# Rotary turn of q in an attention stage: sine parts swapped by transfers and summed on GpSimd, q once in the scores

## The reference

```python
h = rmsnorm(x) * ln1_w                   # queries from x
q = rope(h @ Wq)                         # 16 heads of 64
k = rope(rmsnorm(ctx) * ln1_w @ Wk)      # 4 heads of 64
v = rmsnorm(ctx) * ln1_w @ Wv
x = x + softmax(q k^T / 8 + mask) v @ Wo # 4 query heads share a k head
m = rmsnorm(x) * ln2_w
x = x + (silu(m @ Wgate) * (m @ Wup)) @ Wdown
rope(a) = a * cos + rotate_half(a) * sin # rotate_half(a) = [-a2, a1]
```

## Time and profile before

| | |
|---|---|
| median of 3 runs | 496.73 us (496.45 to 497.52) |
| the profiled execution's own time | 496.65 us |
| its span, first to last instruction | 494.7 us |
| TensorE busy | 445.4 us (90%) |
| VectorE busy | 381.2 us (77%) |
| ScalarE busy | 299.3 us (60%) |
| GpSimd busy | 273.8 us (55%) |

### The profile page before, as it was taken

How to read it: one execution, slowest core, us unless ns; L and a number is a source line. 1 busy time by engine, 2 the same in 40 slices (tenths; PEclk the granted TensorE clock), 3 DMA queues, 4 the chain that set the end, 5 groups by cost and what they waited for, 6 DMA issues and landing times.

```text
span 494.7 us, 16947 instructions
## 1 busy us (share of the span) xinstructions
PE 445.4 (90%) x6872; PEld 353.1 (71%) x6872; DVE 381.2 (77%) x918; ACT 299.3 (60%) x725; POOL 273.8 (55%) x332
## 2 busy tenths in 40 slices
PE   4698899999999999989989768999999999999876
PEld 4466666666666676679877656888888888878664
DVE  6699877688988888968889878877686876767632
ACT  2377676768676877666863655576656665544431
POOL 6464887579867787965644374454353535421210
PEclk9799999999999999999999999999999999999998
DMA  8960000000000000000000000000000000000000
GB/s 291 240 234 3 2 3 3 2 3 3 1 3 2 3 3 3 3 1 2 1 1 3 2 1 4 3 12 2 14 1 13 1 3 14 1 13 1 14 2 21
DMA packets 12421, 11.54 MB, mean 23 GB/s; under 512 B 5177, under 2 KB 10297, under 8 KB 12345
## 3 DMA queue, kind: packets, MB, share of 16 engines
q1 hardware_dynamic: 11624, 9.01, 6.7%
q10 hardware_dynamic: 720, 1.45, 0.8%
HBM read 9.42 MB, written 1.05 MB: 21 GB/s over the span
## 4 chain that ended last, share of the span: by engine, by line
PE 51%; DVE 24%; issue 14%; POOL 5%; ACT 4%; DMA 1%; DVEq 0%; POOLq 0%; ACTq 0%
DVE negm L1249 8%; PE ps L618 5%; DVE blocks L1240 5%; PE ps L634 4%; PE ps L656 4%; PE ps L448 4%; PE ps L734 4%; PE ps L466 3%; PE ps L532 2%; PE ps L545 2%; PE ps L611 2%; PE ps L626 2%; PE ps L496 2%; PE ps L664 2%; PE ps L408 2%
## 5 line engine op out<-in xcount | busy, mean ns | idle before, releaser
L1249 DVE TENSOR_REDUCE negm<-ps 128x8 bf16<-128x512 f32 x96 | 59.6, 683 | 24.9 <-PE ps L448 24.8
L833 ACT ACTIVATE p<-ps 128x512 f32<-128x512 f32 x96 | 54.7, 595 | 27.5 <-PE ps L456 26.4
L839 ACT ACTIVATE shared<-ps 128x512 f32<-128x512 f32 x96 | 57.0, 601 | 21.8 <-PE ps L466 20.4
L1742 POOL TENSOR_TENSOR wide<-wide,cv 128x1024 f32<-128x1024 f32 x24 | 45.5, 1896 | 32.8 <-ACT wide L823 32.8
L466 PE MATMUL ps<-cst,p 128*128 128x128 f32 x384 | 58.4, 276 | 0.4 <-ACT shared L839 0.4
L1795 POOL TENSOR_TENSOR probs<-p,rc 128x512 f32<-128x512 f32 x32 | 33.4, 1057 | 43.2 <-DVE rc L1535 43.1
L1669 POOL TENSOR_TENSOR rstd<-veps,neghalf 128x2 f32<-128x2 f32 x40 | 29.3, 732 | 46.4 <-DVE veps L1285 28.2
L466 PEld LDWEIGHTS ps<-cst,p 128*128 128x128 f32 x384 | 44.2, 141 | 11.5 <-issue 9.4
L1028 ACT ACTIVATE late<-ps 128x512 f32<-128x512 f32 x32 | 17.3, 594 | 34.3 <-PE ps L757 34.3
L618 PE MATMUL ps<-shared,wq 128*128 128x256 f32 x128 | 31.3, 386 | 5.2 <-ACT shared L976 3.4
L634 PE MATMUL ps<-wo,late 128*128 128x128 f32 x256 | 31.5, 276 | 4.0 <-ACT late L1028 3.8
(11 more groups left out here) (204 smaller groups left out, 1150.9 us busy)
## 6 DMA issues: line engine op xcount, KB each, us to landing
late<-in_mask_l SPq DMA_DIRECT2D x2, 512.0 KB, 11.0
result<-x_all SPq DMA_DIRECT2D x8, 128.0 KB, 1.8
x_all<-in_x_tok SPq DMA_DIRECT2D x1, 768.0 KB, 6.6
...
wa<-in_wa SPq DMA_DIRECT2D x1, 512.0 KB, 8.4
w<-in_w SPq DMA_DIRECT2D x2, 256.0 KB, 7.5
wq<-in_wq SPq DMA_DIRECT2D x1, 512.0 KB, 7.2
```

The lines of the kernel that those rows point to most:

```text
L833: A_(p3[:, n % 3, :], ps[:, S_BANK[r], :], ACT.Exp, scale=SC8).then_inc(sm["act_exp"], 1)
L839: A_(pt[:, w % 2, r, :], pt_bank(RG * w + r), ACT.Copy).then_inc(sm["act_pt"], 1)
L1249: V.tensor_reduce(negm[:, n % 4, :], ps[:, S_BANK[r], :].rearrange("p (a k) -> p a k", k=S), AX.X, ALU.max, negate=True).then_inc(sm["dve_ ...
L1742: P.tensor_tensor(r_op[:, w % 2, :, :], k_t[:, w % 2, :].unsqueeze(1).to_broadcast([128, 4, GT]), head_masks.unsqueeze(2).to_broadcast([12 ...
```

## The change

q is turned in full. VectorE multiplies each of `q0` to `q3` twice, 512 columns each: by sine into `q_sin` and by cosine into `q3`. For each two of them four transfers on SP's queue (`a` = 0: q0 and q1; `a` = 1: q2 and q3), of 32 partitions x 1024 columns, move the sine parts between the halves of a head into `q_swap`. GpSimd adds `q_swap` to the cosine parts (`turn_q`). `ks`, `kcs`, two of the three sums in `sum_k` and half the small matmuls go. q2 and q3 stand directly behind the scores of the second half; the opening has another order on all engines. Epsilon additions and small scalings that were `tensor_scalar` are `tensor_reduce` over a pair of columns, of which one holds epsilon. The sum over the context is split in two, in passes 6 and 7; `masks` goes from pass 4 to 5.

```diff
         HALVES = (
             (("s0", 0), ("s1", 0), ("pv0", -1), ("pv1", -1), ("l_in", 2), ("md", -2), ("l_text", 2), ("k", 2), ("out", -1),
              ("l_gate", 2), ("t0", 0), ("in", 1), ("t1", 0), ("q0", 1), ("q1", 1)),
-            (("s0", 0), ("s1", 0), ("pv0", -1), ("pv1", -1), ("m_in", -1), ("kt", 2), ("ks", 2), ("q2", 1), ("q3", 1),
+            (("s0", 0), ("s1", 0), ("q2", 1), ("q3", 1), ("pv0", -1), ("pv1", -1), ("m_in", -1), ("kt", 2),
              ("out", -1), ("v", 2), ("mg0", -1), ("mu0", -1), ("l_back", 2), ("t0", 0), ("mg1", -1), ("mu1", -1), ("t1", 0)),
         )
         OPENING = (
-            (("s0", 0), ("s1", 0), ("l_in", 2), ("s0", 1), ("s1", 1), ("in", 1), ("k", 2), ("v", 2), ("l_text", 2),
-             ("t0", 0), ("q0", 1), ("q1", 1), ("t1", 0), ("l_gate", 2)),
-            (("q2", 1), ("q3", 1), ("kt", 1), ("ks", 1), ("pv0", -1), ("pv1", -1), ("t0", 0), ("out", -1), ("t1", 0),
-             ("l_back", 2)),
+            (("l_in", 2), ("v", 2), ("l_text", 2), ("in", 1), ("l_gate", 2), ("s0", 0), ("s1", 0), ("q0", 1), ("q1", 1),
+             ("s0", 1), ("s1", 1), ("q2", 1), ("q3", 1), ("k", 2), ("t0", 0), ("t1", 0)),
+            (("kt", 1), ("pv0", -1), ("pv1", -1), ("l_back", 2), ("t0", 0), ("out", -1), ("t1", 0)),
         )
...
+            def swap_halves(g):
+                half = HD3 // 2
+                for a in range(2):
+                    eng.wait_ge(sm["q_sin"], 4 * g + 2 * a + 2)
+                    if g >= 1:
+                        eng.wait_ge(sm["q_rot"], 4 * (g - 1) + 2 * a + 2)
+                    two = slice(2 * a, 2 * a + 2)
+                    for i in range(4):
+                        to, of = half * i, half * (i ^ 1)
+                        eng.dma_start(q_swap[to:to + half, two, :], q_sin[of:of + half, two, :])\
+                           .then_inc(sm[f"q_swap{a}"], 16)
...
             for g in range(NG):
+                if g + 2 < NG:
+                    swap_halves(g + 2)
                 eng.wait_ge(*released("md", g))
...
-                    for c in range(2):
-                        for i in range(2):
...
+                    if u == 0:
+                        if a == 0:
+                            pe.wait_ge(*released("kt", g))
+                        pe.wait_ge(sm["q_rot"], 4 * g + 2 * a + 2)
...
+            def q_times(g, i, to, c):
+                tab = cst[:, C_ROPEQ + c * S:C_ROPEQ + c * S + S].unsqueeze(1).to_broadcast([128, 2 * GB, S])
+                return V.tensor_tensor(to, bank_of(f"q{i}", g).rearrange("p (b q) -> p b q", q=S), tab, ALU.mult)
+
+            def sine(g, a):
+                if g >= 1:
+                    dve.wait_ge(sm[f"q_swap{a}"], 64 * g)
+                for i in range(2 * a, 2 * a + 2):
+                    dve.wait_ge(sm["p_use"], filled(f"q{i}", g))
+                    q_times(g, i, q_sin[:, i, :].rearrange("p (b q) -> p b q", q=S), 1).then_inc(sm["q_sin"], 1)
...
             def opening():
-                smax3(0)
                 rms_mean(1)
+                rotate_k(1)
+                l2_max(2)
+                smax3(0)
                 smax3(1)
+                sine(1, 0)
                 sum3(0)
                 sum3(1)
-                rotate_k(1)
-                smax3(2)
-                smax3(3)
                 read("q0", 1)
                 read("q1", 1)
+                smax3(2)
+                l2_gate(2)
+                smax3(3)
+                sine(1, 1)
+                read("q2", 1)
+                read("q3", 1)
+                l2_weigh(2)
                 sum3(2)
                 sum3(3)
-                l2_max(2)
-                read("q2", 1)
-                read("q3", 1)
-                l2_gate(2)
+                rotate_k(2)
                 read("out", 0)
-                rotate_k(2)
-                l2_weigh(2)
                 ffn_rows(NG - 2)
...
             def second_half(r):
...
                 if r + 1 < NG:
+                    sine(r + 1, 0)
                     read("q0", r + 1)
                     read("q1", r + 1)
+                    sine(r + 1, 1)
                 if live:
                     smax3(2 * n)
                     smax3(2 * n + 1)
...
+            def turn_q(g, i):
+                pool.wait_ge(sm[f"q_swap{i // 2}"], 64 * (g + 1))
+                pool.wait_ge(*released(f"q{i}", g))
+                P.tensor_tensor(q_rows(g, i), q_rows(g, i), q_swap[:, i, :].rearrange("p (b q) -> p b q", q=S), ALU.add)\
+                    .then_inc(sm["q_rot"], 1)
...
             def opening():
+                turn_q(0, 0)
+                turn_q(0, 1)
                 rms_power(1)
+                turn_q(0, 2)
+                turn_q(0, 3)
+                sum_k(1)
                 probs3(0)
                 probs3(1)
-                sum_k(1)
+                l2_logits(2)
+                turn_q(1, 0)
+                turn_q(1, 1)
                 probs3(2)
                 probs3(3)
-                l2_logits(2)
                 l2_fuse(2)
+                turn_q(1, 2)
+                turn_q(1, 3)
                 sum_k(2)
...
             def second_half(r):
+                if r + 1 < NG:
+                    turn_q(r + 1, 0)
+                    turn_q(r + 1, 1)
                 if r + 2 < NG:
                     l2_fuse(r + 2)
                 if r < NG:
                     probs3(4 * r + 2)
                     probs3(4 * r + 3)
+                if r + 1 < NG:
+                    turn_q(r + 1, 2)
+                    turn_q(r + 1, 3)
...
-                V.tensor_scalar(veps[:, gs, :], mv[:, gs, :, 1], LN_EPS, None, ALU.add).then_inc(sm[s + "ve"], 1)
+                V.tensor_reduce(veps[:, gs, :], mv[:, gs, :, 1:3], AX.X, ALU.add).then_inc(sm[s + "ve"], 1)
...
-                if w == 2:
...
-                if w == 4:
+                if w == 5:
                     masks()
+                if w in (6, 7):
+                    visual_sums(w - 6)
```

More of the change, by code:

```diff
@@ L281, in build @@
         UNITS = (*PER_UNIT, "out")
-        BY_ACT = ("in", "l_in", "l_text", "l_gate", "l_back", "k", "kt", "ks", "v", "m_in")
+        BY_ACT = ("in", "l_in", "l_text", "l_gate", "l_back", "k", "kt", "v", "m_in")
         def half(r, h):
@@ L596, in part_in @@
                     src = [hm[:, g % 2, i, :] for i in range(TG)]
-                elif what in ("kt", "ks"):
-                    if what == "kt":
-                        pe.wait_ge(sm["d_kr"], g + 1)
-                    else:
-                        pe.wait_ge(sm["d_ks"], 2 * g + 2)
-                    src = [(kc if what == "kt" else kcs)[:, i, a * 128:a * 128 + 128] for a in range(2) for i in range(TG)]
+                elif what == "kt":
+                    pe.wait_ge(sm["d_kr"], g + 1)
+                    src = [kc[:, i, a * 128:a * 128 + 128] for a in range(2) for i in range(TG)]
                 elif what == "l_in":
@@ L688, in fill @@
                 take_bank(what, g)
-                if what in ("in", "m_in", "kt", "ks", "l_in", "l_back"):
+                if what in ("in", "m_in", "kt", "l_in", "l_back"):
                     ins = part_in(what, g)
@@ L1032, in opening @@
                 A_(first_exp[:, :], neghalf[:, 0:1], ACT.Exp)
+                read("l_in", 2)
+                read("v", 2)
+                read("l_text", 2)
                 sq3(1)
-                read("l_in", 2)
+                rms(1)
+                read("in", 1)
+                read("l_gate", 2)
                 exps3(0)
-                rms(1)
                 exps3(1)
-                read("in", 1)
-                read("k", 2)
-                read("v", 2)
-                evac_t3(0)
-                read("l_text", 2)
+                l2_exp(2)
                 exps3(2)
                 exps3(3)
+                read("k", 2)
+                evac_t3(0)
                 evac_t3(1)
-                read("l_gate", 2)
                 read("kt", 1)
-                read("ks", 1)
-                l2_exp(2)
+                l2_tanh(2)
                 evac_pv3(0)
                 evac_pv3(1)
+                read("l_back", 2)
                 evac_t3(2)
-                l2_tanh(2)
-                read("l_back", 2)
             def first_half(r):
@@ L1073, in first_half @@
                     read("kt", 2)
-                    read("ks", 2)
                 if live:
@@ L1113, in second_half @@
                 if r + 2 < NG:
-                    read("ks", r + 2)
                     read("v", r + 2)
@@ L1142, in _ @@
             read("kt", 0)
-            read("ks", 0)
             f_in(6)
@@ L1181, in ln0 @@
                     dve.wait_ge(sm["ln0_mv"], 4 * g + 1 + t)
-                    V.bn_aggr(mv[:, g % 2, t, :], st[:, g % 2, t, :]).then_inc(sm["ln0_mv"], 1)
+                    V.bn_aggr(mv[:, g % 2, t, 0:2], st[:, g % 2, t, :]).then_inc(sm["ln0_mv"], 1)
                 dve.wait_ge(sm["ln0_mv"], 4 * g + 4)
```

(12 more changed lines are left out.)

100 lines of the change are left out of this document (47 added, 53 removed).

## The result

The changed kernel takes 512.81 us (median of 4 runs, 510.74 to 514.26), the kernel before in the same session 496.67 us: ratio 1.032, 95% interval 1.029 to 1.035. It is 3.2% slower; the prediction said 1.0% faster. The profiled execution took 510.74 us (span 508.2), the lowest of the four.

What follows compares the result with a forecast made beforehand. It took TensorE to bound the last stage's rounds, with VectorE nearly gapless in their second half. +0.5 - 1.5 - 0.4 + 1.0 - 2.0 - 0.6 - 2.0 = -5.0 us on 496.65 gave 491.7 us, range 485 to 500.

Steps and rivals of the forecast that it cites:

- rival 1: Last stage: a slow swap makes GpSimd's queue the bound; 502 us at L = 6; chance 0.22.
- L: Last stage: latency of the four swap transfers from the end of sine until the last lands, taken as 3.8 us.
- the opening, +1.0: Opening and round 1: q0 of round 1 comes 1.0 us late, the half after it as long as before.
- rival 3: All is given back: opening +3 us by port waits, l2_weigh losing a turn each round; 495.7, up to 496.9; chance 0.14.
- rounds near 27.3: Last stage: sign of the forecast, a round near 27.3 us against 27.8 before.
- -2.0 as forecast: Rounds 2 to 5: 0.5 us saved in each, -2.0 us together.
- a port wait of `l2_weigh`: Second half of a round: l2_weigh on VectorE waits for GpSimd's turn 1 to end, costing 0.5 us.
- to L = 4.5 the slack holds: GpSimd's queue in the rounds: swap latency up to 4.5 us delays nothing; beyond, each us costs one in each of seven swaps.
- 0 to 1 us: GpSimd's queue in a round: turns, l2_fuse, probs3 and l2_rstd all fit, with 0 to 1 us to spare.
- Rounds 6 and 7, -2.6 forecast: Last two rounds: -0.6 us in round 6, -2.0 in round 7, where both scores lie on the way to the end.
- Ahead of the last stage, -1.4: Before the last stage: pooled sum and masks +0.5, veps as reductions -1.5, ks transposes gone -0.4 us.
- Rival 2: Rounds: VectorE gets off the line TensorE follows, 9.4 us more saved, 482 us; chance 0.12.

Runs made afterwards that it cites:

- e6: The changed kernel with another opening order (l_gate ahead of in(1), group 2's gate chain and l_back sooner): 506.45 us, ratio 1.019.
- e7: e6 plus matmuls of no use in three waits of the opening (16, 10 and 8): 505.18 us, ratio 1.014.
- e3: The changed kernel with 60 matmuls of no use in four long TensorE waits of the opening: 506.34 us, ratio 1.018.
- e1: The kernel before with only the small edits (epsilons by reductions, pooled sum split, masks in pass 5): 496.91 us, ratio 0.999.
- e8: The kernel before with 14 and 6 matmuls of no use ahead of l_back(2) and l_text(3): 495.77 us, ratio 0.998.
- e4: The changed kernel with turn_q of groups 0 and 1 done on one block of 64 columns instead of 8: 511.11 us, ratio 1.028.
- e5: The changed kernel with transfers made, but turn_q adds q_sin in place and doesn't wait for them: 504.33 us, ratio 1.016.
- e15: The changed kernel with l2_tanh ahead of evac_pv3, l2_weigh ahead of smax3, l2_fuse ahead of turns 0 and 1: 506.83 us, ratio 1.020.
- e2: The changed kernel without the swap's transfers; turn_q adds q_sin in place: 505.47 us, ratio 1.017.
- e16: The changed kernel with the reorders of e6 and e15 and matmuls of no use in the opening's waits: 496.04 us, ratio 0.999.

## Why the prediction was wrong

**Direction.** Forecast 491.7 in 485 to 500, measured 512.8. No case on record reached it, rival 1 (502 at L = 6) least far off.

**The step that failed is the opening, +1.0 for 14.3 measured.** The walk followed two engines, VectorE's sum of work (285.5) and GpSimd's behind it, as if TensorE only joined in at the end, with nothing for TensorE's idle time and nothing for its clock. Four things were not in it; in the profiles they add up as 3.6 + 6.2 + 1.7 + 2.8.

- *The order on TensorE and the two-engine steps between.* I had the scores of unit 0 over at 270.2; they ended at 275.4. `in` (1) stands ahead of `l_gate`, of the scores and of all q, and waits for the normalised x of group 1 (hn): turns 0 and 1 ahead of `rms_power` (which then takes 1.15 us by the port, with `l2_rows` at 1.64), ScalarE 0.7, so 269.1. `l_gate` needed none of that. Behind it the chain `l_gate`, `l2_exp`, `l2_gate`, `l2_logits`, `l2_weigh`, `l2_fuse`, `l_back` ran late into TensorE's list, ahead of `out` and unit 2. e6 against after gives 6.5 us, clock included; with the waits filled 3.6 are left (e7 against e3, less the first q).
- *The clock behind the waits.* The text said nothing of it. 6.2 us (e3 against after).
- *The clock in the first q.* 1.6 to 1.7 us, in the profile of after and not in that of before. Whether the change makes it more frequent isn't shown: it is in 11 of the 17 profiles with after's code up to there, and in none of the three (before, e1, e8) with the old one.
- *What is left*: 2.8 us (e7's 47.4 against 44.6, both at full clock), put down to the added work because nothing else is left. It is close to rival 3's price for the opening, +3 by port waits. Of it the turns are some 1 us (e4 against e5 and e15, in the old order); the eight more products over q were not tried by themselves.

**Rounds.** Without the swap's wait they take 27.30 us; "rounds near 27.3" was the forecast, and `mg0` and `mu0` are preceded by the 0.25 us that VectorE's q2 and q3 end. In the main this walk was right: 0.5 us in each of rounds 2 to 5, -2.0 as forecast, and 1.1 more in round 1, where nothing was forecast. That it is just 0.5 is in part luck: it was to be 1.0 in the first half less a port wait of `l2_weigh`. In e2 that instruction takes 0.41 us and waits for no port; the first half is 0.8 us shorter and the second 0.3 longer. The swap then costs 5.6 us in the profile of after (141.5), 7.4 in those of e3, e4 and e6 (143.3), and 7.5 and 7.8 by the ratios of e2 and e5. The step that failed is "to L = 4.5 the slack holds". L was 4.3, the forecast 3.8: the fourth issue started 1.9 us after the sine and not 1.3, since issues follow at 0.6 us and not at 0.42, and it landed 2.3 us later and not the store's 1.8. That alone is within the 4.5, yet turns 0 and 1 ran from 7.9 to 10.6 after q0 and not from 6.9 to 9.5 (the sine ended at 3.6 and not 3.0), and the slack of "0 to 1 us" was used up there. Rival 1's mechanism is what happened, from a lower threshold: the turns, then `l2_rstd`, then `l2_norm`, and by the port `l2_weigh` too, which takes 0.42 us where no turn stands in its way and 0.8 to 1.4 where one does. Which rounds it hits differs from profile to profile.

The Trainium skill, "DMA: Bandwidth & Descriptors", section "Anatomy of one DMA", gave an estimate of 3.6 us for the last of four; L was 4.3. The section's figures are for transfers that GpSimd issues, and these were SyncE's. For one transfer its sum would be 2.3 us, and the trace has 2.3 for SyncE's too. What was short is the 1.3 us for the row of issues, which came from a row of the kernel before.

**Rounds 6 and 7, -2.6 forecast.** The masks of the last unit stand 23.5 us behind q0 of round 6 before and 23.4 after: nothing gained up to there. The whole stretch is 55.7 before, but 54.1 in e8 with the same code. The difference is the clock at the very end, first before, then e8:

```profile
480.00:494.70 14.70, 8.76 (x43) 6.96 (x41) 3.77 (x7) 2.59 (x7) 0.69 (x1) 0.88 0.06 18
```

```profile
480.00:492.90 12.90, 6.95 (x42) 5.66 (x40) 3.77 (x7) 2.45 (x6) 0.70 (x1) 1.00 0.07 20
```

With a clock of 1.00 from 480 on, after has 53.0 and e16 53.0 against e8's 54.1: 1.1 us of the 2.6 came. What holds the rest was not tried.

**Ahead of the last stage, -1.4 with the `ks` transposes.** Each step came as walked (`smax` at 68.24, `veps` at 0.16 us), but e1, which has these edits without the `ks` transposes, gives -0.5 us in an interval from -1.3 to +0.3: its -1.0 can't be told from nothing, nor be ruled out. q0 of group 0 starts between 253.7 and 256.6 in profiles of the same code up to there, so the lead of 0.6 in the table above says nothing.

**The rivals.** Rival 2 (VectorE off the line) did not happen: with everything else taken out, rounds stayed at 27.3. Rival 3 had the port waits right and no idle TensorE in it. That no rival named the opening's waits or the clock is why none came near 512.8.
